# Loads of the quarter layout: one DMA per block of 32 rows to all 128 partitions, instead of one per 32 partitions, nearly all on SP's queue

## What is computed

```python
Bx   = einsum('bni,bri->bnr', x, cond_B[ids])          # ids: one adapter per batch
cond = einsum('bnr,bor->bno', Bx, cond_A[ids])
base = einsum('bsi,oi->bso', cond, base_w) + base_b
hid  = einsum('bsi,ri->bsr', cond, ffn_A)
probs = softmax(einsum('bsi,ei->bse', cond, router_w))
topw, topi = top_k(probs, 2); topw = topw / (sum(topw) + 1e-6)
combine = sum(one_hot(topi, 16) * topw[..., None], axis=-2)
delta = einsum('bse,bsr,eor->bso', combine, hid, ffn_B)
out = x + base + 0.5 * delta
```

## Time and profile before

| | |
|---|---|
| median of 3 runs | 505.19 us (502.99 to 508.53) |
| profiled execution | 510.71 us, span 508.8 us |
| PE busy | 413.9 us (81%) |
| DVE busy | 285.6 us (56%) |
| ACT busy | 111.9 us (22%) |
| DMA, mean | 266 GB/s, 135.29 MB |

### The profile page before, as it was taken

One profiled execution on the slowest core, in us unless ns is written; L12 is line 12 of the kernel. 1 busy time (PEld: TensorE's weight loads), 2 busy tenths in 40 slices (PEclk: granted clock), 3 DMA queues, 4 the chain that ended last, 5 costly groups with the idle time before them and its releaser, 6 DMA issues.

```text
span 508.8 us, 5807 instructions
## 1 busy us (share of the span) xinstructions
PE 413.9 (81%) x2112; PEld 250.6 (49%) x2112; DVE 285.6 (56%) x627; ACT 111.9 (22%) x174; POOL 47.9 (9%) x54
## 2 busy tenths in 40 slices
PE   0000199889399669999999999999999999999997
PEld 0000056344154335755675665576567566557665
DVE  1100077765147257677567676776756767677543
ACT  0000343525155111210230230121023023112210
POOL 3003310000002000120120030012012003001200
PEclk9999999989699979999999999999999999999999
DMA  8999934949848939999999999999999999935754
GB/s 232 219 272 287 307 99 126 331 169 287 242 164 286 333 123 259 252 375 290 276 340 327 281 336 354 247 294 360 280 294 356 311 268 321 363 126 177 280 226 166
DMA packets 93331, 135.29 MB, mean 266 GB/s; under 512 B 13620, under 2 KB 46388, under 8 KB 93300
## 3 DMA queue, kind: packets, MB, share of 16 engines
q1 hardware_dynamic: 66932, 107.64, 69.0%
q10 hardware_dynamic: 26370, 27.27, 21.6%
HBM read 99.24 MB, written 35.65 MB: 265 GB/s over the span
## 4 chain that ended last, share of the span: by engine, by line
PE 67%; ACTq 11%; DVE 10%; DMA 9%; issue 2%; ACT 1%; DVEq 0%
PE ps L776 11%; PE ps L793 11%; PE ps L794 9%; PE ps L795 9%; PE ps L741 8%; DMA early_u<-in_L_ffn_B 6%; PE ps L807 6%; PE ps L796 5%; ACTq L243 4%; PE ps L731 3%; ACTq L227 3%; DVE xT L612 3%; DVE h_r L602 3%; DMA g_hilo<-u_r 2%; ACTq L427 2%
## 5 line engine op out<-in xcount | busy, mean ns | idle before, releaser
L719 DVE TENSOR_TENSOR xbuf<-ps,xbuf 128x512 f32<-128x512 f32 x128 | 86.9, 679 | 106.2 <-PE ps L796 105.9
L793 PE MATMUL ps<-h_r,u_r 128*128 128x512 f32 x256 | 109.8, 429 | 14.0 <-DVE xbuf L719 14.0
L794 PE MATMUL ps<-h_r,u_r 128*128 128x512 f32 x256 | 100.7, 394 | 0.0
L795 PE MATMUL ps<-h_r,u_r 128*128 128x512 f32 x256 | 100.5, 393 | 0.0
L741 PE MATMUL ps<-early 128*128 128x512 f32 x128 | 71.0, 645 | 35.0 <-ACT early L418 33.7
L562 DVE STREAM_TRANSPOSE early<-xbuf 128x512 f32<-128x512 f32 x64 | 43.2, 692 | 81.7 <-PE ps L741 66.8
L793 PEld LDWEIGHTS ps<-h_r,u_r 128*128 128x128 f32 x256 | 48.3, 189 | 55.6 <-DVE xbuf L719 21.6
L612 DVE STREAM_TRANSPOSE xT<-xbuf 128x512 f32<-128x512 f32 x112 | 72.0, 681 | 0.0
L776 PE MATMUL ps<-bexpT,cur 128*32 128x512 f32 x512 | 61.8, 600 | 2.1 <-DVE h_r L602 2.1
L418 ACT ACTIVATE h_r<-ps 128x512 fp32r<-128x512 f32 x64 | 35.7, 594 | 109.6 <-issue 66.1
L731 PE MATMUL ps<-ident,early_u 128*128 128x128 f32 x128 | 25.6, 293 | 40.1 <-DMA early_u<-in_L_ffn_B 40.1
(11 more groups left out here) (63 smaller groups left out, 215.6 us busy)
## 6 DMA issues: line engine op xcount, KB each, us to landing
xbuf<-in_x SPq DMA_DIRECT2D x32, 1024.0 KB, 7.9
out<-xbuf SPq DMA_DIRECT2D x31, 1024.0 KB, 6.8
xbuf<-in_x SPq DMA_DIRECT2D x28, 512.0 KB, 11.0
xbuf<-in_x ACTq DMA_DIRECT2D x28, 512.0 KB, 9.4
xbuf<-in_L_ffn_base_w SPq DMA_DIRECT2D x8, 1024.0 KB, 13.4
xbuf<-in_L_ffn_base_w ACTq DMA_DIRECT2D x8, 1024.0 KB, 17.8
early_u<-in_L_ffn_B SPq DMA_DIRECT2D x16, 512.0 KB, 9.5
gm_r<-g_hilo SPq DMA_DIRECT2D x128, 32.0 KB, 6.5
```

What stands on the lines that cost most here:

```text
L719: dve.tensor_tensor(xs, ps[:, ACC + t % 2, :], xs, ALU.add).then_inc(s_out, 1)
L793: pe.matmul(acc, u_r[:, b.q, 0, h, tok_t], hi, start=(h == 0), stop=False)
L794: pe.matmul(acc, u_r[:, b.q, 0, h, tok_t], lo, start=False, stop=False)
L795: pe.matmul(acc, u_r[:, b.q, 1, h, tok_t], hi, start=False, stop=False)
```

## The change

All loads in the quarter layout (base_w, cond_B, ffn_A, and x) are cut the other way. Before, one DMA took one quarter q of all blocks t to 32 partitions. Now one DMA takes one block t of 32 rows, all four quarters of it, to all 128 partitions. A W group is 16 DMAs of 256 KB instead of 4 of 1 MB, a batch of x is 32 of 128 KB instead of 8 of 512 KB, cond_B 4 of 256 KB, ffn_A 2 of 256 KB. The x of the first batch gets a layout with rows of 512 columns and comes as 16 DMAs of 256 KB. `load_gm` takes both parts of G in one DMA of 64 KB instead of two of 32 KB. ACT keeps only the token ids and 24 of the 32 loads of cond_A. Bytes and contiguous rows are the same as before (2 KB for W, 1 KB for the x of batches 1 to 7), but for the first batch's x, whose rows are now 2 KB.

```diff
-    w_q = base_w.rearrange("(g t l) (q d) -> g q l t d", t=BANK // SQ, l=SQ, q=NQ)
+    w_q = base_w.rearrange("(g t l) (q d) -> g t q l d", t=BANK // SQ, l=SQ, q=NQ)
...
-    condb_v = cond_B.rearrange("n k d -> (n k) d").rearrange("(t l) (q d) -> q l t d", l=SQ, q=NQ)
-    ffna_v = ffn_A.rearrange("(t l) (q d) -> q l t d", l=SQ, q=NQ)
-    x_q = x.rearrange("b (t l) (q g d) -> b g q l t d", l=SQ, q=NQ, g=2)
+    condb_v = cond_B.rearrange("n k d -> (n k) d").rearrange("(t l) (q d) -> t q l d", l=SQ, q=NQ)
+    ffna_v = ffn_A.rearrange("(t l) (q d) -> t q l d", l=SQ, q=NQ)
+    x_q = x.rearrange("b (t l) (q g d) -> b g t q l d", l=SQ, q=NQ, g=2)
+    x_0 = x[0].rearrange("(t l) (q d) -> t q l d", l=SQ, q=NQ)
...
-        def load_xquad(eng, b, g, qs, where=None):
-
-            for q in qs:
-                eng.dma_start((xquad if where is None else where)[q * SQ:(q + 1) * SQ, g], x_q[b, g, q])\
-                   .then_inc(s_xquad[g], 16)
...
+        def load_xquad(eng, b, g):
+
+            for t in range(T // SQ):
+                eng.dma_start(xquad[:, g, t, :], x_q[b, g, t]).then_inc(s_xquad[g], 16)
+
+        def load_w(eng, g):
+
+            for t in range(BANK // SQ):
+                eng.dma_start(w_part(g)[:, t, :], w_q[g, t]).then_inc(s_load[W_BUF[g]], 16)
...
-                    for l in range(2):
-                        row = (2 * rep + l) * RK
-                        sp.dma_start(f32(gm_r[row:row + RK, c * BANK:(c + 1) * BANK]),
-                                     g_dram[l, bass.ds(b * RK, RK), c * BANK:(c + 1) * BANK]).then_inc(s_gm[c], 16)
...
+                    sp.dma_start(f32(gm_r[rep * 2 * RK:(rep + 1) * 2 * RK, c * BANK:(c + 1) * BANK]),
+                                 g_dram[:, b * RK:(b + 1) * RK, c * BANK:(c + 1) * BANK]).then_inc(s_gm[c], 16)
...
-            act.dma_start(tok[:, :], itok.rearrange("(a b) -> a b", a=1)).then_inc(s_tok, 16)
-            load_w(act, 0, (2, 3))
-            load_cond_a(act, range(NAD // 2, NAD))
...
+            load_cond_a(act, range(2, NAD))
```

More of the change, by code:

```diff
@@ L271, in load_gm @@
                 for rep in range(2):
-                    for l in range(2):
-                        row = (2 * rep + l) * RK
-                        sp.dma_start(f32(gm_r[row:row + RK, c * BANK:(c + 1) * BANK]),
-                                     g_dram[l, bass.ds(b * RK, RK), c * BANK:(c + 1) * BANK]).then_inc(s_gm[c], 16)
[L277 to L281, removed]
-                load_expert(e)
-            for row in (64, 96):
-                sp.dma_start(bias_n[row:row + 1, :], base_b.rearrange("(a o) -> a o", a=1)).then_inc(s_bias, 16)
+                    sp.dma_start(f32(gm_r[rep * 2 * RK:(rep + 1) * 2 * RK, c * BANK:(c + 1) * BANK]),
+                                 g_dram[:, b * RK:(b + 1) * RK, c * BANK:(c + 1) * BANK]).then_inc(s_gm[c], 16)
+            load_w(sp, 0)
+            load_cond_a(sp, range(0, 2))
+            for e in range(3):
+                load_expert(e)
+            for t in range(P // SQ):
+                sp.dma_start(condb_q[:, t, :], condb_v[t]).then_inc(s_condb, 16)
+            load_w(sp, 1)
+            load_expert(3)
+            for t in range(T // SQ):
+                sp.dma_start(xquad0[:, t, :], x_0[t]).then_inc(s_x0, 16)
+            for e in range(4, 6):
+                load_expert(e)
+            for t in range(R // SQ):
+                sp.dma_start(ffna_q[:, t, :], ffna_v[t]).then_inc(s_small, 16)
             sp.wait_ge(s_const, 1)
@@ L288, in _ @@
                   .then_inc(s_small, 16)
[L289 to L292, removed]
+            for row in (64, 96):
+                sp.dma_start(bias_n[row:row + 1, :], base_b.rearrange("(a o) -> a o", a=1)).then_inc(s_bias, 16)
+            load_expert(6)
             sp.wait_ge(s_wt, KD)
-            load_w(sp, 2, (0, 1))
+            load_w(sp, 2)
             load_expert(7)
@@ L336, in step @@
                         xquad_free(sp, f, c)
-                        load_xquad(sp, f.n + 1, c, range(0, NQ // 2))
+                        load_xquad(sp, f.n + 1, c)
                     if c > 0:
@@ L465, in h_hi, with slot @@
                     copy(h_r[:, c % 2, 0, h, :], ps[:, HB + h, :]).then_inc(s_hhi, 1)
[L467 to L470, removed]
+            def slot(f, m):
                 if m == BXP_AT:
@@ L498, in _ @@
             for n in range(NW):
-                if n % KD == NEXT_W_AT % KD and 2 <= n // KD + 1 < W_GROUPS:
-                    act.wait_ge(s_wt, n // KD * KD)
-                    load_w(act, n // KD + 1, (2, 3))
                 if n >= GHI_AT and n % KD == GHI_AT % KD:
                     g_hi(n // KD - 1)
[L504 to L507, removed]
                 for e in expert_done(n):
@@ L512, in _ @@
                         act.wait_ge(s_gst, 16 * (W_GROUPS - 1))
-                    slot(first, SLOT_AT[n], False)
+                    slot(first, SLOT_AT[n])
             g_hi(W_GROUPS - 1)
@@ L603, in h_lo, with x_transpose @@
                                       ALU.subtract).then_inc(s_hlo, 1)
-            def x_transpose(f, j, where):
+            def x_transpose(f, j):
                 g, i = j // (KD // 2), j % (KD // 2)
-                if i == 0:
-                    dve.wait_ge(s_xquad[g], f.n * 16 * NQ + 16 * NQ)
+                if f.n == 0:
+                    src = xquad0[:, :, j * SQ:(j + 1) * SQ]
+                    if j == 0:
+                        dve.wait_ge(s_x0, T // SQ * 16)
+                else:
+                    src = xquad[:, g, :, i * SQ:(i + 1) * SQ]
+                    if i == 0:
+                        dve.wait_ge(s_xquad[g], f.n * (T // SQ) * 16)
                 if j == 0:
@@ L695, in _ @@
                         dve.wait_ge(s_biaslo, 1)
-                    x_transpose(first, X_AT[n], xquad0)
+                    x_transpose(first, X_AT[n])
                 if n >= GLO_AT and n % KD == GLO_AT % KD:
```

26 lines of the change are left out of this document (11 added, 15 removed).

## The result

The changed kernel takes 884.0 us (median of 4 runs, 883.74 to 886.43) against 506.86 us: a ratio of 1.75, with a 95% interval of 1.737 to 1.762. The forecast was 860 us, slower, in a range of 770 to 1110.

A forecast was written before the change was run, and what follows sets the result against it. PE set the pace before, with DMA engines nearly full; after, engine 0 would. Setup to 349 us, six steps of 75.8 us and an unchanged 72.3 us tail, with small corrections, gave span 859 and forecast 860 us, range 770 to 1110.

The forecast's parts named there:

- How many engines share a load: In the changed loads the smaller leading count decides: four engines for a quarter load, two for `gm`, the same each time.
- The first rival: All 16 engines still share each load, DMA time as before: about 500 us, between 490 and 508; chance 0.08.
- the second: Rival: four engines per load but not the same four, so the load evens out; about 505 us; chance 0.03.
- The steps: In each of six steps that load x, engine 0 has 75.8 us of work against PE's 42.5; nothing hides the excess.
- the landing of the reload: At the step's start, the reload of `xres` chunk 0, awaited by DVE's first add, was given 2 us to land.
- Setup: From the start to the first store of a chunk: 349 us, some 162 us behind the kernel before.
- The last W group: In setup, W group 3 was to land at 275 us and its 16 transposes to end at 296, taking 21 us.
- the experts: Expert loads on SP's queue in setup, 0.52 MB over 16 engines, were priced at 1.4 us each.
- The x of batch 1 and the store behind it: End of setup: x takes 43.3 us, and with the last store of G behind it this ends at 342 us.
- The last two steps: At the end of the kernel, without x quarters: as before, 72.3 us, giving a span of 859 us.
- The range: 770 to 1110 us; the forecast with rates from 19.3 GB/s to 12% over 24.9 was given chance 0.80.
- The price of a byte: The busiest engine moves 24.2 GB/s, bounds 19.3 and 13.3 below, 12% over 24.9 above; 743 us go by this rate.

The follow-up runs named there:

- experiments 1: The changed kernel with its quarter loads cut to lead with 32 on both sides, same size and nearly same number, `gm` loads still leading with 2: 618.34 us, ratio 1.224.
- 5: The changed kernel with each x load of batches 1 to 7 cut into two of 64 KB whose DRAM side leads with 2: 1188.02 us.
- 3: The kernel before the change with the `gm` loads alone in the changed form, leading with 2: 563.72 us, ratio 1.113.
- 4: The changed kernel with the x loads of batches 1 to 7 alone cut to lead with 32, the rest left narrow: 736.1 us.

## Why the prediction was right, and where it was off

- **How many engines share a load** was the step that decided. It was read from packet counts of the kernel before and from the smaller of two leading counts; experiments 1 and 5 show it at 32, 4 and 2, and the packet total came out within one. The first rival (all 16 share) is excluded by the same count, the second (four, but not the same) by the share of 0.26 at 102 GB/s with several W loads in flight, and by the 77 us of a step.
- **The steps.** 75.8 us were worked out, 77.0 measured: 1.835 MB at 23.8 instead of 24.2 GB/s. Six steps made that 7 us. About 5 more are left over; the landing of the reload, for which I allowed 2 and which took 10 (issued at 492.69 us, DVE's add at 502.78), would cover them, but this wasn't separated. What is late is `xres` chunk 0, as said.
- **Setup.** 349 us to the first store were worked out, 365.5 measured. ffn_A was turned at 162.11 instead of 168, as W came at 25.5 GB/s an engine. The last W group was to be transposed from 275 to 296 and was from 285.94 to 308.48: the term that was too small is the experts. Expert 12 was issued at 266.77, behind the whole group, and PE stood for it 33.58 us, until 281.10; expert 7, issued at 208.75 behind group 2, held PE in the same way. The chain of the kernel before had two such waits, 15 and 17 us, and I had priced an expert by its bytes (1.4 us) and not by its place in the queue. The 21 us for the last 16 transposes came out as 22.5, since they were read from SP's issue at 143.13 us, which came 2 us after the first of them. The x of batch 1 and the store behind it took 50 us (358.83 - 308.48) instead of 46.
- **The last two steps** took 3 us less than before (884.6 - 820.70 = 63.9 against 66.9). Together: 16.5 + 12 - 3 = 25.5, from 859 to the span of 884.6.
- **The range.** At 12% over 24.9 GB/s the working gives 762 and not "about 770"; the measured time is far from either.
- **The price of a byte** held for what it was used for, narrow loads with the 12 other engines silent or partly busy. It did not hold for what I then expected of experiments 1, 3 and 4, where all 16 are active: 18.4 to 19.8 GB/s. The bound of 19.3 that the prediction kept for the range was the right value for those. Had I looked at the kernel before in this way, it would have said that its own steps had no room for `gm` either. The two rates of an engine are measured; what makes the difference (the HBM, or stores mixed in) was not separated.

## What to carry to other kernels

Before a load is reshaped, look at the outermost count of its pattern on *both* sides: the smaller one bounded how many engines carried it in every load seen here, whatever the destination looked like, and counting completion packets in a profile tells which it was. Then look at which partitions the transfers in flight at one time go to: two queues, or two halves of one queue's order, should be in different halves of the 128. And if the DMA shares are near 1 beside a full PE, a load of 3% of the bytes that goes to two engines is enough to set the pace.

## What the runs showed of the hardware

- A load whose DRAM side leads with 4 or 2 and whose SBUF side leads with 128 or 64 is carried by 4 or 2 engines, the same ones each time: 96 to 102 GB/s at shares of 0.26 and 0.27 with 4, 48 GB/s at 0.14 with 2, and steps of 77.0 and 121.0 us.
- One engine moves 24.0 GB/s with 1 KB rows and 25.5 with 2 KB rows while 12 others are nearly silent. In steps in which all work and stores are mixed in it is 18.4 to 19.8 GB/s, worked out as the bytes of engine 0 over the length of the step. I had not expected the second to be lower than the first by a quarter.
- Loads by 16 engines that all go to one half of the partitions run at 190 to 220 GB/s at shares of 1.11 and 1.12; spread over both halves 327 GB/s (share 1.09). A share near 1 thus doesn't tell how much is moved.
